# Channel mix's second product in the search rounds: three products of rounded parts, in portions by pairs of chunks

## The chip, the cores and the metric

The kernel runs on one core of a Trainium2 chip. The metric is the time of one execution on the device in microseconds (us), as the median of several runs. Engine names in the profile: PE is TensorE (PEld its weight loads), DVE is VectorE, ACT is ScalarE, POOL is GpSimd, SP is SyncE.

## The reference, cut to what matters

The input is 16 sequences of 512 tokens with 256 channels. Each token goes through an RWKV block, and beside it through a mixture of 8 experts whose SiLU gates the block's output. The part that is changed is channel mix:

```
xk2 = h2 * cmk + shift(h2) * (1 - cmk)
kf  = square(relu(xk2 @ Wfk.T))        # 1024 hidden channels
kv  = kf @ Wfv.T                       # the second product, 1024 -> 256
x   = x + sigmoid(xr2 @ Wfr.T) * kv
```

Beside the blocks the kernel routes tokens: each expert takes its 1024 most probable tokens, and for that the threshold of each expert is searched bit by bit.

## The kernel before, in words

A block is one sequence of 512 tokens; there are 16 (NB). The kernel goes through rounds 0 to 15. In round b each engine works on three blocks at once: channel mix of block b - 1, the output projection and second norm of block b, and the first norm, mixes and projections of block b + 1. Rounds 3 to 11 also carry the routing: round 3 the softmax, rounds 4 to 10 (BIT_ROUND to SELECT_ROUND - 1) four bits of the threshold search each, round 11 (SELECT_ROUND) the choice of tokens. From round 12 (LIST_ROUND) on GpSimd writes the sorted token list with indirect DMAs. After round 15 the expert stage follows.

Each engine executes its own instructions in the order in which they are written; engines wait for each other on semaphores. The order within a round is written out by hand in each engine's round_. On TensorE it is: hidden (channel mix's first product, L937 to L944, eight chunks of 128 hidden channels, each of which ScalarE takes out of psM by a ReLU, L642), the bit search's small matmul (sum_bit, L837), receptance (L956), turn1 (transposes for block b + 1, L870), channel_out portion 0 (L968), project_out (L919), projections of k and v (L905), channel_out portion 1, turn2, projection of r, channel_out portions 2 and 3.

Portion j of channel_out is a quarter of the tokens over all eight chunks, in full precision, which needs two instructions for each of its eight matmuls; portion 0 waits until all eight chunks are squared (sq_done, L646). Its result is in psKV; VectorE takes it in the next round (gate_out, L1542).

VectorE's round is: state scans (L1453), embedding (L1558, L1563), a bit test (try_bit, L1210 to L1217), L1460, L1542, statistics (L1375, L1379), L1549, the recurrence's mixes (L1471 to L1500), a bit test, the token-shift mixes (L1392, L1396), the residual after the output projection (L1533), statistics, a bit test, L1396, scans (L1439 to L1447), a bit test, and the second block's mixes (L1392, L1396, L1431). ScalarE's round is logs (L620), ReLUs and squares with the Tanh pairs (L626, L629) between them, the first norm (norm1, L545), more ReLUs and squares, affine1 (L553), the Tanh of the receptance (L654), taking the projections (L592, L590), the second norm, norm0 (L536), affine2, Exp (L603), L598, the rounded copies of the mix (L635), Exp (L608). GpSimd's round is rstd1 and rstd2 only: four small operations of 4 elements a partition each (L441, L442, L444, L446), on which norm1 and norm2 wait.

The first product already works with rounded parts: the high part is a copy to the type float32r (mix_hi), the low part is the difference (mix_lo), and hi x hi, hi x lo and lo x hi are summed. The expert stage's second product does the same with 256 columns (L1062 to L1064).

Of the kernel before, what the change touches and what calls it, by code (L numbers as in the profile page):

```python
# [27 lines left out]
F32 = mybir.dt.float32  # L28
I32 = mybir.dt.int32
F32R = mybir.dt.float32r  # L30
ALU = mybir.AluOpType
ACT = mybir.ActivationFunctionType
# [3 lines left out]
P = 128  # L36
ROUTER_ROUNDS = 3
BIT_ROUND = 4
SELECT_ROUND = BIT_ROUND + 7
LIST_ROUND = SELECT_ROUND + 1  # L40
# [30 lines left out]
def rwkv_times_moe(nc, x, xT, vec, ln0_w, ln0_b, WkT, WvT, WrT, WoT, WfkT, WfrT, WfvT, Wg, W1, W2,  # L71
                   consts, tile_iota, token_ids, pad_rows, sorted_list, xs_rows, out):
    T, C = x.shape
    SEQ = 512
    NB = T // SEQ
# [16 lines left out]
    with ExitStack() as ctx:  # L92
# [7 lines left out]
        def same_place(name, words, other, first=0):  # L100
            return nc.alloc_sbuf_tensor_at(name, [P, words], F32R, offset=home[other] + 4 * first)
# [50 lines left out]
        def part(n):  # L152
            at[0] += n
            assert at[0] <= ARENA
            return arena[:, at[0] - n:at[0]]
# [15 lines left out]
        x_in_at = at[0]  # L171
        x_in = part(J * C).rearrange("p (j c) -> p j c", j=J)
        mixB_r = part(CH * SEQ).rearrange("p (c t) -> p c t", c=CH)
        kf2 = part(HC * SEQ).rearrange("p (h t) -> p h t", h=HC)
        moe_end = at[0]
        sigf = part(J * C)
        wfr = part(CH * C).rearrange("p (k n) -> p k n", k=CH)
        wfk = kf2.rearrange("p h t -> p (h t)")[:, 0:CH * HID].rearrange("p (k n) -> p k n", k=CH)
        wfv = part(HC * C).rearrange("p (k n) -> p k n", k=HC)
        xa = [desk[:, i * 1024:(i + 1) * 1024].rearrange("p (j c) -> p j c", j=J) for i in range(2)]  # L180
        xta = [desk[:, 2048 + i * 1024:3072 + i * 1024].rearrange("p (k t) -> p k t", k=CH) for i in range(2)]
        ra = 4096
# [63 lines left out]
        h1_ready mix1_step mix1_done mixr1_done proj_done kvr_ready wkv_step pre_done relu2_done exp_done att_done o_done  # L246
        state_done log_done gap_done past_done now_done
        x2_done ln2_step ln2_stats cf2_ready hn2_ready tr2_done h2_ready mix2_step mixk_done mixk_hi wfk_hi_done mix2_done mixr2_done
        kf_done relu_done sq_done fr_done sigf_done kv_done s_done s_mult rstd1_step rstd2_step
        rows_zeroed s_idx_ready xn_done turned w1_taken xn_taken h_done gelu_done h_hi_done h_lo_done y_done tanh_done  # L250
        combine_step combined""".split()
        names += [f"{n}{i}" for n in ("gathered", "s_gathered") for i in range(RING)] + [f"rows_out{i}" for i in range(RING)]
# [6 lines left out]
        def wait_run(eng, s, value):  # L259


            eng.wait_ge(s, value)
            if not isinstance(value, int):
                eng.sem_inc(S["waited"])
# [129 lines left out]
        def _(pool):  # L394
# [60 lines left out]
            def zero_rows():  # L455
# [2 lines left out]
                    ins = pool.memset(rows[i], 0.0)  # L458
                ins.then_inc(S["rows_zeroed"], 1)

            def round_(b, listing=False, ahead=True):
                if ahead:
                    rstd1(b + 1)
                if listing:
                    add_to_list(b, 0)
                if not ahead:
                    add_to_list(b, 1)
                rstd2(b)
                if not ahead:
                    zero_rows()  # L470
                if listing and ahead:
                    add_to_list(b, 1)
# [7 lines left out]
                norm_scales(b + 1, 4 * b, 4 * b + 3)  # L480
                rstd2(b)
            norm_scales(ROUTER_ROUNDS + 1, NB - 4, NB - 1)
            with pool.Fori(ROUTER_ROUNDS, LIST_ROUND) as b:
                round_(b)
            round_(LIST_ROUND, listing=True)
            with pool.Fori(LIST_ROUND + 1, NB - 1) as b:
                round_(b, listing=True)
# [41 lines left out]
        def _(act):  # L529
# [33 lines left out]
            def affine1(b):  # L563

                if not (isinstance(b, int) and b < 2):
                    wait_run(act, S["mixr2_done"], b - 1)
                affine(b, "tr1_done", "ln1_w", "ln1_b", "h1_ready")

            def norm2(b):

                if not (isinstance(b, int) and b == NB - 1):
                    wait_run(act, S["tr1_done"], b + 2)
                norm(b, cf2, "cf2_ready", "hn2_ready")
# [26 lines left out]
            def exp_past(b):  # L600

                wait_run(act, S["pre_done"], b * CH + CH)
                act.activation(E1, E1, ACT.Exp).then_inc(S["exp_done"], 1)  # L603
# [6 lines left out]
            def keep_logits(k):  # L610

                act.wait_ge(S["logits_done"], 4 * k + 4)
                act.activation(logits[:, k * 4 * J * E:(k + 1) * 4 * J * E], psR[:, 0:4 * J * E], ACT.Copy
                               ).then_inc(S["logits_kept"], 1)
# [29 lines left out]
            def square(b, h):  # L644
                act.wait_ge(S["relu_done"], b * HC + (h + 1))
                act.activation(kf2[:, h], kf2[:, h], ACT.Square).then_inc(S["sq_done"], 1)  # L646

            def sigmoid_fr(b):

                if not (isinstance(b, int) and b == 0):  # L650
                    wait_run(act, S["s_done"], b)
                for u in range(2):
                    act.wait_ge(S["fr_done"], 2 * b + (u + 1))
                    act.activation(sigf[:, u * 512:(u + 1) * 512], psM[:, (HC + u) % 3, :],  # L654
                                   ACT.Tanh, scale=0.5).then_inc(S["sigf_done"], 1)

            def relus(b, *chunks):
                for h in chunks:
                    relu(b, h)

            def squares(b, *chunks):
                for h in chunks:
                    square(b, h)

            def round_(b, ffn=True, ahead=True, softmax=False, further=True):
                logs(b)
                if not ffn:
                    keep_logits(0)
                if ffn:
                    for h in range(2):  # L670
                        relus(b - 1, h)
                        squares(b - 1, h)
                    relus(b - 1, 2)
                shares(b)
                if ffn:
                    relus(b - 1, 3, 4)
                    squares(b - 1, 2)
                    relus(b - 1, 5)
                if ahead:
                    norm1(b + 1)  # L680
                if ffn:
                    relus(b - 1, 6)
                    squares(b - 1, 3)
                    relus(b - 1, 7)
                    squares(b - 1, 4, 5, 6, 7)
                if softmax:
                    act.wait_ge(S["route_exp_in"], 1)
                    act.activation(probs, logits, ACT.Exp).then_inc(S["route_exp_out"], 1)
                if ahead:
                    affine1(b + 1)  # L690
                if isinstance(b, int) and b == 1:
                    keep_logits(2)
                if ffn:
                    sigmoid_fr(b - 1)
                else:
                    act.wait_ge(S["weights_in"], 16 * 3)
                    act.activation(wfk_hi[:], wfk, ACT.Copy).then_inc(S["wfk_hi_done"], 1)
                if ahead:
                    take_kvr(b + 1, 0, 2)
                if not ffn:  # L700
                    keep_logits(1)
                norm2(b)
                if ahead:
                    take_kvr(b + 1, 2, 4)
                    if further:
                        norm0(b + 2)
                affine2(b)
                if ahead:
                    exp_past(b + 1)
                    take_kvr(b + 1, 4, 5)  # L710
                    exponents(b + 1)
                split_mix(b, 0)
                split_mix(b, 1)
                if ahead:
                    exp_now(b + 1)
                    take_kvr(b + 1, 5, 6)
# [14 lines left out]
            for b in range(1, ROUTER_ROUNDS):  # L731
                round_(b)
            round_(ROUTER_ROUNDS, softmax=True)
            with act.Fori(BIT_ROUND, NB - 2) as b:
                round_(b)
            round_(NB - 2, further=False)
            round_(NB - 1, ahead=False)
# [70 lines left out]
        def _(pe):  # L808
# [160 lines left out]
                                    wfv[:, h, :], start=(h == 0), stop=(h == HC - 1))  # L969
                ins.then_inc(S["kv_done"], 1)  # L970

            def round_(b, extra, ffn=True, ahead=True):
                if ffn:
                    hidden(b - 1, extra, b)
                    receptance(b - 1)
                else:
                    extra(b, 0)
                if ahead:
                    turn1(b + 1)
                if ffn and ahead:  # L980
                    channel_out(b - 1, 0)
                project_out(b)
                if ffn and not ahead:
                    channel_out(b - 1, 0)
                extra(b, 1)
                if ahead:
                    project(b + 1, 0, 1)
                if ffn:
                    channel_out(b - 1, 1)
                turn2(b)  # L990
                extra(b, 2)
                if ahead:
                    project(b + 1, 2)
                if ffn:
                    channel_out(b - 1, 2)
                extra(b, 3)
                if ffn:
                    channel_out(b - 1, 3)
# [14 lines left out]
                round_(b, router_point)  # L1013
            round_(ROUTER_ROUNDS, softmax)
            with pe.Fori(BIT_ROUND, SELECT_ROUND) as b:
                round_(b, sum_bit)
            round_(SELECT_ROUND, route)
            with pe.Fori(LIST_ROUND, NB - 1) as b:
                round_(b, nothing)
            round_(NB - 1, nothing, ahead=False)  # L1020
# [709 lines left out]
```

## Time and profile before

| what | value |
|---|---|
| median of 3 runs | 1076.61 us (1076.31 to 1077.09) |
| the profiled execution | 1077.64 us |
| its span in the profile | 1075.8 us |
| PE busy | 1015.7 us, 94% |
| DVE busy | 882.0 us, 82% |
| ACT busy | 689.6 us, 64% |
| POOL busy | 383.4 us, 36% |

Busy shares are averages over stages; what bounds a round is read from the waits in it. A row of the timeline gives start and length in us, engine, line and operation, output and input, and how many instructions the row merges; brackets give the idle time before it and who ended it. A full-precision matmul appears as two instructions.

### The profile page before, as it was taken

The numbers are of one execution on the slowest core, as the hardware profiler recorded it, in microseconds if no ns is written. First come the engines' busy times: TensorE is split into PE (matmuls) and PEld (weight loads), VectorE is DVE, ScalarE is ACT, GpSimd is POOL, SyncE is SP. The second block draws the span as 40 slices with busy tenths as digits, with TensorE's granted clock in tenths as the row PEclk, the third lists the DMA queues.
The fourth block names the chain that finished last, engine by engine and source line by source line (L and its number), as shares of the span: only waits on it lengthen the run. The fifth ranks groups of instructions, "written<-read, shape, count | busy, mean of one in ns | idle before, by whom it ended". The sixth has DMA issues, their size and how long they took to land.

```text
span 1075.8 us, 18544 instructions
## 1 busy us (share of the span) xinstructions
PE 1015.7 (94%) x5410; PEld 832.7 (77%) x5410; DVE 882.0 (82%) x1763; ACT 689.6 (64%) x1231; POOL 383.4 (36%) x407
## 2 busy tenths in 40 slices
PE   4899999899999999999999969999999999999996
PEld 4578787677777767777776757777788999999996
DVE  5899898998988889898899987887665777777775
ACT  2558567585857658585765557595555666666663
POOL 3204055110101021010101045656762776666663
PEclk9889999999999999999999989999999999999998
DMA  7544320101102010110101020124361433333320
GB/s 257 168 141 120 98 79 20 40 7 54 58 0 58 0 58 15 43 58 0 58 0 59 1 59 1 59 68 129 120 223 40 122 122 114 113 114 109 108 67 21
DMA packets 59473, 80.28 MB, mean 75 GB/s; under 512 B 7678, under 2 KB 46719, under 8 KB 59394
## 3 DMA queue, kind: packets, MB, share of 16 engines
q1 hardware_dynamic: 48130, 54.16, 15.9%
q0 software_dynamic: 11280, 25.32, 7.9%
q8 instruction: 35, 0.57, 0.2%
q14 instruction: 28, 0.23, 0.1%
HBM read 64.38 MB, written 26.36 MB: 84 GB/s over the span
## 4 chain that ended last, share of the span: by engine, by line
PE 59%; DVE 19%; issue 9%; ACT 7%; POOL 4%; DMA 1%; DVEq 1%; SPq 0%; ACTq 0%; POOLq 0%
PE psKV L968 12%; PE psM L1042 11%; PE psM L905 11%; PE psM L919 5%; DVE arena L1453 2%; DVE arena L1396 2%; ACT arena L646 2%; PE psT L870 2%; ACT arena L545 2%; DVE bnst L1375 2%; PE psM L937 2%; PE psM L956 2%; PE psKV L1062 2%; POOL cf L444 2%; PE psKV L1064 1%
## 5 line engine op out<-in xcount | busy, mean ns | idle before, releaser
L968 PE MATMUL psKV<-arena 128*128 128x256 f32 x1024 | 231.2, 380 | 2.6 <-ACT arena L646 2.6
L968 PEld LDWEIGHTS psKV<-arena 128*128 128x128 f32 x1024 | 192.7, 190 | 42.0 <-issue 17.5
L441 POOL TENSOR_SCALAR lnw<-mv 128x4 f32<-128x4 f32 x32 | 19.0, 593 | 519.2 <-DVE mv L1379 519.2
L1042 PE MATMUL psM<-arena 128*128 128x128 f32 x1136 | 139.5, 276 | 1.5 <-DVE arena L1630 1.4
L1042 PEld LDWEIGHTS psM<-arena 128*128 128x128 f32 x1136 | 132.2, 192 | 3.2 <-DVE arena L1630 2.5
L937 PE MATMUL psM<-mix_hi,wfk_hi 128*128 128x512 f32 x256 | 107.8, 421 | 21.2 <-ACT arena L642 21.2
L592 ACT ACTIVATE arena<-psM 128x512 f32<-128x512 f32 x64 | 36.5, 588 | 127.9 <-PE psM L905 127.9
L1396 DVE SCALAR_TENSOR_TENSOR arena<-arena,vecs 128x512 f32<-128x512 f32 x160 | 109.9, 745 | 0.1
L507 POOL DMA_INDIRECT out_dram<-arena,list_sb x71 | 86.5, 1218 | 59.1 <-DVE arena L1661 50.4
L545 ACT ACTIVATE arena<-s_ring,cf 128x256 f32 (+1 forms) x128 | 66.4, 591 | 59.9 <-POOL cf L446 59.9
L939 PE MATMUL psM<-mix_hi,wfk_lo 128*128 128x512 f32 x256 | 102.3, 400 | 0.0
L642 ACT ACTIVATE arena<-psM 128x512 f32<-128x512 f32 x128 | 73.7, 587 | 28.9 <-PE psM L944 26.4
L768 ACT ACTIVATE arena<-psM 128x512 f32<-128x512 f32 x71 | 42.5, 599 | 63.2 <-PE psM L1042 63.2
L434 POOL DMA_INDIRECT sorted_list<-info_cur,place_cur x64 | 73.7, 1151 | 22.3 <-issue 20.6
L944 PE MATMUL psM<-mix_lo,wfk_hi 128*128 128x512 f32 x256 | 80.9, 398 | 0.0
L937 PEld LDWEIGHTS psM<-mix_hi,wfk_hi 128*128 128x128 f32 x256 | 49.7, 194 | 36.5 <-ACT arena L642 26.8
L646 ACT ACTIVATE arena<-arena 128x512 f32<-128x512 f32 x128 | 75.2, 624 | 1.0
L494 POOL DMA_INDIRECT arena<-xs_rows,list_sb x62 | 65.9, 1063 | 21.0 <-issue 18.6
L956 PE MATMUL psM<-arena 128*128 128x256 f32 x256 | 60.4, 383 | 4.6 <-ACT arena L642 4.6
L905 PE MATMUL psM<-arena,wk 128*128 128x512 f32 x128 | 61.5, 626 | 0.5 <-DVE arena L1396 0.5
L919 PE MATMUL psM<-wo,arena 128*128 128x256 f32 x256 | 59.4, 386 | 0.7 <-DVE arena L1500 0.5
L1392 DVE TENSOR_TENSOR arena<-arena 128x512 f32<-128x512 f32 x64 | 41.7, 688 | 22.0 <-ACT arena L553 21.9
(212 smaller groups left out, 2368.4 us busy)
## 6 DMA issues: line engine op xcount, KB each, us to landing
arena<-in_x SPq DMA_DIRECT2D x16, 512.0 KB, 4.1
desk<-in_xT SPq DMA_DIRECT2D x16, 512.0 KB, 4.1
xs_rows<-s_ring SPq DMA_DIRECT2D x16, 512.0 KB, 3.2
xs_rows<-in_x SPq DMA_DIRECT2D x16, 512.0 KB
desk<-in_x SPq DMA_DIRECT2D x15, 512.0 KB, 5.0
desk<-in_W SPq DMA_DIRECT2D x8, 512.0 KB, 8.4
arena<-in_W SPq DMA_DIRECT2D x8, 512.0 KB, 7.3
out_dram<-arena,list_sb POOLq DMA_INDIRECT x71, 2.7
```

Of the source, the lines that this page charges most:

```text
L507: pool.indirect_dma_start(out[:, :], bass.IndirectOffsetOnAxis(list_sb[:, t, 0:1], axis=0), out_t[i], None, bounds_check=T - 1, oob_is_err ...
L545: ins = act.activation(hn[:, j], xs[:, j * C:(j + 1) * C], ACT.Identity, scale=cf[:, 0, j:j + 1], bias=cf[:, 1, j:j + 1])
L646: act.activation(kf2[:, h], kf2[:, h], ACT.Square).then_inc(S["sq_done"], 1)
L905: ins = pe.matmul(psM[:, u % 3, :], w[:, k, c * P:(c + 1) * P], mixA[:, m, k, :], start=(k == 0), stop=(k == CH - 1))
L919: ins = pe.matmul(psM[:, 1 + j // 2, (j % 2) * C:(j % 2 + 1) * C], att[:, c, j * P:(j + 1) * P], wo[:, c, :], start=(c == 0), stop=(c == C ...
L937: pe.matmul(psM[:, h % 3, :], wfk_hi[:, k, n], mix_hi[:, k, :], start=(k == 0), stop=False)
L939: pe.matmul(psM[:, h % 3, :], wfk_lo[:, k, n], mix_hi[:, k, :], start=False, stop=False)
L944: ins = pe.matmul(psM[:, h % 3, :], wfk_hi[:, k, n], mix_lo[:, k, :], start=False, stop=(k == CH - 1))
L956: ins = pe.matmul(psM[:, (HC + u) % 3, (j % 2) * C:(j % 2 + 1) * C], mixB_r[:, k, j * P:(j + 1) * P], wfr[:, k, :], start=(k == 0), stop=( ...
L968: ins = pe.matmul(psKV[:, j // 2, (j % 2) * C:(j % 2 + 1) * C], kf2[:, h, j * P:(j + 1) * P], wfv[:, h, :], start=(h == 0), stop=(h == HC ...
L1042: ins = pe.matmul(psM[:, t % 2, f * P:(f + 1) * P], w1_t[t % 2][:, k, f * P:(f + 1) * P], xnT[t % 2][:, k, :], start=(k == 0), stop=(k == ...
L1396: return v.scalar_tensor_tensor(dst[:, c], dmix[:, c], vecs[:, c, V[m]:V[m] + 1], hT[:, c, 0:SEQ], ALU.mult, ALU.add)
```

## The change

In rounds 4 to 11 (so for blocks 3 to 10) channel_out is replaced by channel_part. Portion p is now a pair of hidden chunks (2p, 2p + 1) over all 512 tokens. It has 24 matmuls of 256 columns: for each of four token groups and two chunks hi x hi and hi x lo, then, behind a second wait, lo x hi. Each portion waits for its own high part (ScalarE, take_hi: one copy of 128x1024 to float32r) and its own low part (GpSimd, take_lo: one subtraction of 128x1024). The low part replaces the chunk in place; the high part goes to four slots in desk. The weights wfv are split once: ScalarE copies the high part in round 3, GpSimd subtracts in place (128x2048) once round 3's product is done, and adds the parts together again (128x2048) once round 11's product is done; TensorE waits for that at the start of round 12. ScalarE's squares 4 to 7 move from behind ReLU 7 to places after the receptance's Tanh and after the first two projections.

```diff
+            def take_lo(b, p):
+                wait_run(pool, S["kf_hi_done"], (b - BIT_ROUND) * J + (p + 1))
+                n, slot = slice(2 * p, 2 * p + 2), 2 * (p % 2)
+                pool.tensor_tensor(kf_lo[:, n], kf2[:, n], kf_hi[:, slot:slot + 2].bitcast(F32), ALU.subtract
+                                   ).then_inc(S["kf_lo_done"], 1)
+
+            def split_wfv():
+                pool.wait_ge(S["wfv_hi_done"], 1)
+                pool.wait_ge(S["kv_done"], J * ROUTER_ROUNDS)
+                pool.tensor_tensor(wfv_lo, wfv, wfv_hi.bitcast(F32), ALU.subtract).then_inc(S["wfv_lo_done"], 1)
+
+            def join_wfv():
+                pool.wait_ge(S["kv_done"], J * SELECT_ROUND)
+                pool.tensor_tensor(wfv, wfv_lo.bitcast(F32), wfv_hi.bitcast(F32), ALU.add).then_inc(S["wfv_whole"], 1)
+
+            def parts_round(b):
+                rstd1(b + 1)
+                take_lo(b, 0)
+                take_lo(b, 1)
+                rstd2(b)
+                take_lo(b, 2)
+                take_lo(b, 3)
...
-            with pool.Fori(ROUTER_ROUNDS, LIST_ROUND) as b:
-                round_(b)
+            round_(ROUTER_ROUNDS)
+            split_wfv()
+            with pool.Fori(BIT_ROUND, LIST_ROUND) as b:
+                parts_round(b)
+            join_wfv()
...
+            def take_hi(b, p):
+                act.wait_ge(S["sq_done"], b * HC + (2 * p + 2))
+                act.wait_ge(S["kv_done"], b * J + (p - 1))
+                slot = 2 * (p % 2)
+                act.activation(kf_hi[:, slot:slot + 2], kf2[:, 2 * p:2 * p + 2], ACT.Copy).then_inc(S["kf_hi_done"], 1)
...
+                if parts:
+                    take_hi(b - 1, 0)
                 if ahead:
                     norm1(b + 1)
                 if ffn:
                     relus(b - 1, 6)
                     squares(b - 1, 3)
                     relus(b - 1, 7)
-                    squares(b - 1, 4, 5, 6, 7)
+                    if not parts:
+                        squares(b - 1, 4, 5, 6, 7)
...
+                if parts:
+                    squares(b - 1, 4, 5)
+                    take_hi(b - 1, 1)
                 if ahead:
                     take_kvr(b + 1, 0, 2)
...
+                if parts:
+                    squares(b - 1, 6, 7)
+                    take_hi(b - 1, 2)
                 norm2(b)
...
                     exp_past(b + 1)
+                    if parts:
+                        take_hi(b - 1, 3)
                     take_kvr(b + 1, 4, 5)
...
+            def channel_part(b, p):
+                if p == 0:
+                    pe.wait_ge(S["wfv_lo_done"], 1)
+                    wait_run(pe, S["s_mult"], b)
+                done = b * J - (BIT_ROUND - 1) * J + (p + 1)
+                pe.wait_ge(S["kf_hi_done"], done)
+                out = lambda j: psKV[:, j // 2, (j % 2) * C:(j % 2 + 1) * C]
+                for j in range(J):
+                    for h in (2 * p, 2 * p + 1):
+                        hi = kf_hi[:, h % 4, j * P:(j + 1) * P]
+                        pe.matmul(out(j), hi, wfv_hi[:, h, :], start=(h == 0 and j % 2 == 0), stop=False)
+                        pe.matmul(out(j), hi, wfv_lo[:, h, :], start=False, stop=False)
+                pe.wait_ge(S["kf_lo_done"], done)
+                for j in range(J):
+                    for h in (2 * p, 2 * p + 1):
+                        ins = pe.matmul(out(j), kf_lo[:, h, j * P:(j + 1) * P], wfv_hi[:, h, :],
+                                        start=False, stop=(h == HC - 1 and j % 2 == 1))
+                ins.then_inc(S["kv_done"], 1)
...
             with pe.Fori(BIT_ROUND, SELECT_ROUND) as b:
-                round_(b, sum_bit)
-            round_(SELECT_ROUND, route)
+                round_(b, sum_bit, channel_out=channel_part)
+            round_(SELECT_ROUND, route, channel_out=channel_part)
+            pe.wait_ge(S["wfv_whole"], 1)
```

## Rows read from the trace of the kernel before

**Rows 1.** The page, busy time and share of the span by engine.
```profile
PE 1015.7 (94%) x5410; PEld 832.7 (77%) x5410; DVE 882.0 (82%) x1763; ACT 689.6 (64%) x1231; POOL 383.4 (36%) x407
```

**Rows 2.** Timeline of VectorE, first instruction of four rounds: start, length, what.
```profile
415.43 2.33 DVE L1453 TENSOR_TENSOR_SCAN arena<-arena 128x512 f32<-128x512 f32 x2
462.33 2.33 DVE L1453 TENSOR_TENSOR_SCAN arena<-arena 128x512 f32<-128x512 f32 x2
556.11 2.33 DVE L1453 TENSOR_TENSOR_SCAN arena<-arena 128x512 f32<-128x512 f32 x2
607.04 2.33 DVE L1453 TENSOR_TENSOR_SCAN arena<-arena 128x512 f32<-128x512 f32 x2
```

**Rows 3.** Waits, 418 to 465 us: who for whom, total, times, longest.
```profile
ACT arena L545 <- POOL cf L446: 3.1, 2, 1.9
DVE s_ring L1533 <- PE psM L919: 2.0, 1, 2.0
DVE desk L1210 <- PE psR L837: 0.9, 1, 0.9
PE psM L937 <- ACT arena L642: 0.7, 1, 0.7
PE psM L956 <- ACT arena L642: 0.5, 1, 0.5
PE psKV L968 <- ACT arena L646: 0.3, 1, 0.3
```

**Rows 4.** Timeline of TensorE in round 8, an old portion, what follows, and the next round's first product.
```profile
450.84 3.62 PE L968 MATMUL psKV<-arena 128*128 128x256 f32 x16
454.29 1.04 PE L870 MATMUL psT<-cst,arena 128*128 128x128 f32 x8
...
465.76 0.58 PE L937 MATMUL psM<-mix_hi,wfk_hi 128*128 128x512 f32 x1
```

**Rows 5.** Timeline of TensorE in the expert stage, first and tenth of ten products.
```profile
902.96 0.28 PE L1063 MATMUL psKV<-w_lo,hT_h 128*128 x1
...
904.02 0.28 PE L1063 MATMUL psKV<-w_lo,hT_h 128*128 x1
```

**Rows 6.** Timeline of ScalarE in round 8.
```profile
445.89 0.60 ACT L592 ACTIVATE arena<-psM 128x512 f32<-128x512 f32 x1 [6.88 <-PE psM L905]
456.79 1.05 ACT L603 ACTIVATE arena<-arena 128x1024 f32<-128x1024 f32 x1
```

**Rows 7.** Timelines of GpSimd in rounds 0 and 3, and of VectorE beside it.
```profile
11.24 0.20 POOL L425 TENSOR_TENSOR info<-desk,info 128x4 f32<-128x4 f32 x1
149.85 2.10 POOL L413 TENSOR_TENSOR desk<-desk,info 128x16 f32<-128x16 f32 x1
150.58 1.28 DVE L1500 SCALAR_TENSOR_TENSOR arena<-arena 128x512 f32<-128x512 f32 x2
152.32 0.23 POOL L416 TENSOR_TENSOR desk<-desk,info 128x16 f32<-128x16 f32 x1
185.95 0.22 POOL L424 TENSOR_TENSOR stats<-desk,stats 128x16 f32<-128x16 f32 x1
```

**Rows 8.** Groups of instructions of GpSimd, one line: busy, mean ns of one.
```profile
L458 POOL MEMSET arena<- 128x512 f32 x9 | 4.2, 523 | 0.0
```

**Rows 9.** Timeline of VectorE in round 8.
```profile
420.42 0.14 DVE L1210 TENSOR_SCALAR desk<-desk 128x1 int32<-128x1 int32 x1
428.25 1.28 DVE L1474 SCALAR_TENSOR_TENSOR arena<-arena 128x512 f32<-128x512 f32 x2
436.50 0.14 DVE L1210 TENSOR_SCALAR desk<-desk 128x1 int32<-128x1 int32 x1
457.26 1.29 DVE L1392 TENSOR_TENSOR arena<-arena 128x512 f32<-128x512 f32 x2
```

**Rows 10.** Waits of VectorE, 556 to 607, and of TensorE, 607 to 663.
```profile
DVE s_ring L1533 <- PE psM L919: 1.6, 1, 1.6
PE psM L937 <- ACT arena L642: 10.0, 1, 10.0
```

More of the change, by code:

```diff
@@ L173, in rwkv_times_moe @@
         mixB_r = part(CH * SEQ).rearrange("p (c t) -> p c t", c=CH)
+        kf_at = at[0]
         kf2 = part(HC * SEQ).rearrange("p (h t) -> p h t", h=HC)
@@ L178, in rwkv_times_moe @@
         wfk = kf2.rearrange("p h t -> p (h t)")[:, 0:CH * HID].rearrange("p (k n) -> p k n", k=CH)
+        wfv_at = at[0]
         wfv = part(HC * C).rearrange("p (k n) -> p k n", k=HC)
+        kf_lo = same_place("kf_lo", HC * SEQ, "arena", kf_at).rearrange("p (h t) -> p h t", h=HC)
+        wfv_lo = same_place("wfv_lo", HC * C, "arena", wfv_at).rearrange("p (k n) -> p k n", k=HC)
+        kf_hi = same_place("kf_hi", 4 * SEQ, "desk").rearrange("p (h t) -> p h t", h=4)
+        wfv_hi = same_place("wfv_hi", HC * C, "desk", 4 * SEQ).rearrange("p (k n) -> p k n", k=HC)
         xa = [desk[:, i * 1024:(i + 1) * 1024].rearrange("p (j c) -> p j c", j=J) for i in range(2)]
@@ L248, in rwkv_times_moe @@
         x2_done ln2_step ln2_stats cf2_ready hn2_ready tr2_done h2_ready mix2_step mixk_done mixk_hi wfk_hi_done mix2_done mixr2_done
-        kf_done relu_done sq_done fr_done sigf_done kv_done s_done s_mult rstd1_step rstd2_step
+        kf_done relu_done sq_done kf_hi_done kf_lo_done wfv_hi_done wfv_lo_done wfv_whole fr_done sigf_done kv_done s_done s_mult rstd1_step rstd2_step
         rows_zeroed s_idx_ready xn_done turned w1_taken xn_taken h_done gelu_done h_hi_done h_lo_done y_done tanh_done
@@ L646, in square, with split_wfv @@
                 act.activation(kf2[:, h], kf2[:, h], ACT.Square).then_inc(S["sq_done"], 1)
+            def take_hi(b, p):
[3 more added lines that the diff above has]
+                act.activation(kf_hi[:, slot:slot + 2], kf2[:, 2 * p:2 * p + 2], ACT.Copy).then_inc(S["kf_hi_done"], 1)
+            def split_wfv():
+                act.wait_ge(S["logits_done"], NB)
+                act.wait_ge(S["a_step"], 2 * NB)
+                act.activation(wfv_hi, wfv, ACT.Copy).then_inc(S["wfv_hi_done"], 1)
             def sigmoid_fr(b):
@@ L663, in squares, with round_ @@
                     square(b, h)
-            def round_(b, ffn=True, ahead=True, softmax=False, further=True):
+            def round_(b, ffn=True, ahead=True, softmax=False, further=True, parts=False):
                 logs(b)
@@ L690, in round_ @@
                     affine1(b + 1)
+                if softmax:
+                    split_wfv()
                 if isinstance(b, int) and b == 1:
@@ L733, in _ @@
             round_(ROUTER_ROUNDS, softmax=True)
-            with act.Fori(BIT_ROUND, NB - 2) as b:
+            with act.Fori(BIT_ROUND, LIST_ROUND) as b:
+                round_(b, parts=True)
+            with act.Fori(LIST_ROUND, NB - 2) as b:
                 round_(b)
@@ L970, in channel_out, with round_ @@
                 ins.then_inc(S["kv_done"], 1)
-            def round_(b, extra, ffn=True, ahead=True):
+            def channel_part(b, p):
[16 more added lines that the diff above has]
+                ins.then_inc(S["kv_done"], 1)
+            def round_(b, extra, ffn=True, ahead=True, channel_out=channel_out):
                 if ffn:
```

## The prediction

> **What bounds the kernel now.** I read the busy shares first: TensorE is busy 94% of the span and VectorE 82%, so both are near the limit and neither name alone says what a saving is worth [rows 1]. Then the timeline of the state scans (L1453), which open a round on VectorE: the changed rounds 4 to 10 repeat in 46.9 us (415.43 to 462.33), round 11 takes 50.9 (556.11 to 607.04) [rows 2]. Then the waits inside round 8. TensorE waits 0.7, 0.5 and 0.3 us, each time for ScalarE; VectorE waits 2.0 us for the output projection (L919) and 0.9 us for the counting matmul [rows 3]. So a round is a loop in which TensorE has 1.5 us of slack and VectorE 2.9 us. A VectorE round that waits for no other engine lasts 46.9 - 2.9 = 44.0 us; that is the floor of the round if only TensorE gets faster, and it is the sum that matters if something is added to VectorE.
>
> **TensorE, removed and added.** One portion of the old product is 16 full-precision instructions in 3.45 us (L968 at 450.84, the next line at 454.29) [rows 4]; four portions are 13.8 us a round. The new one is 96 rounded products with 256 columns. The expert stage has the same form: nine of them start within 904.02 - 902.96 = 1.06 us, 0.118 each [rows 5]. 96 x 0.118 = 11.3 us. TensorE saves 2.5 us a round, and the 0.3 us wait for the squares goes as well, since portion 0 needs only two chunks. That is the nearest row and the lower end; the upper end is one old instruction of 256 columns, 3.45 / 16 = 0.216, by which 96 would take 20.7 (rival 4).
>
> How much of that reaches the round? VectorE's residual (L1533), from which the second norm follows, waits for the output projection, ahead of which only portion 0 has become shorter: 3.45 + 0.3 - 24 x 0.118 = 0.9 us. The other portions lie behind waits: with TensorE early, its chunks 6 and the receptance wait for ScalarE's ReLUs, which are behind the Tanh pair and the first norm, both fed by VectorE and GpSimd. So 0.9 us a round is what the faster product can give, not 2.5.
>
> **ScalarE, added.** Four copies of 128x1024 a round. The nearest row is Exp on the same size, 1.05 us [rows 6]; 4.2 us. ScalarE waits twice a round for a norm's scales from GpSimd, 3.1 us together, the longer 1.9 [rows 3]. Copy 0 falls into the shorter, 1.2 us, so nothing. Squares 4 and 5 and copy 1 (2.1 us) move into the 6.88 us idle ahead of 445.89 [rows 6]; squares 6 and 7 and copy 2 (2.1 us) into the 1.9 ahead of the second norm, 0.2 too long, which I leave out. Only copy 3 stands on the way to the mix's high part and the second Exp: up to 1.05, which the 0.9 us gained ahead of it about pays. If that cover were gone it would cost 1.05 a round. The round-3 copy of the weights (2048 elements, about 2 us) also falls into the 6.88.
>
> **GpSimd, added.** Each round has four subtractions of 128x1024; once come two passes over 128x2048 of weights (the split in round 3 to 4, the join between rounds 11 and 12). No row shows such a size. Two-tensor operations that nothing disturbs take 0.20 us for 4 elements a partition and 0.22 to 0.23 for 16 [rows 7]: 1.7 to 2.5 ns an element, so 1.9 to 2.7 us for 1024. The memset, which only writes, gives a lower end: 523 ns for 512, 1.05 us for 1024 [rows 8]. I take 2.1 us for the part that moves data, the middle of the slopes. On its own queue this is harmless: low part 0 can start at 430.9 and TensorE asks for it some 7 us later, and the second norm's scales are asked for (447) 3 us after pass 1 would end.
>
> **The port between VectorE and GpSimd.** This is what decides. At 149.85 GpSimd starts a two-tensor product of 16 elements; the same kind takes 0.23 us at 152.32, this one takes 2.10 and ends at 151.95. In between VectorE ran an unbroken row of instructions with two SBUF operands, the last two of them from 150.58 to 151.86 [rows 7]: GpSimd was through when they were. So the two engines exclude each other for VectorE instructions with two SBUF operands. The trace shows GpSimd as the loser; its own accesses there are too short to show what VectorE loses. A pass over 1024 elements is not short. If VectorE waits for it, each pass costs VectorE 2.1 us; nothing below zero is possible, since it takes no work from VectorE. Do they meet? On the old clock, each behind its copy: pass 0 at about 430.9 (where the 1.2 us wait ends), inside the stretch of two-operand instructions from 428.25 to 436.50; pass 1 at 441 (445.89 - 6.88 + 2.1), inside the mixes; pass 2 at 449 (the second take of the projection, near 447, + 2.1), ahead of mixes and scans; pass 3 at 458 (the first Exp, 456.79, + 1.05), behind L1392 at 457.26 [rows 6, 9]. All four meet.
>
> VectorE then: 44.0 + 4 x 2.1 = 52.4 us a round, and its two waits (2.9 us) are used up in that. Rounds 4 to 10: 7 x (52.4 - 46.9) = 38.5. Round 11 has 1.6 us of waiting left [rows 10]: 8.4 - 1.6 = 6.8. The two passes over the weights, 4.2 us each, start while VectorE is in the scans and embedding: 8.4. Sum 53.7. For TensorE the join costs nothing: it waits 10.0 us in round 12 as it is [rows 10].
>
> The Trainium skill (SBUF — State Buffer, section "SBUF: two separate sides") states a rule against this change: the pair of ports is an exclusive lock, held for the whole instruction by whichever began first, and a VectorE instruction with two SBUF inputs takes part against a GpSimd one that reads SBUF. The trace agrees for the half it can show (2.10 instead of 0.23 us); by that rule the sum is the one above, and without it the time would be the 1070 of the third rival. The skill's page GPSIMD Engine Reference, section 3.1, gives 4497 ns for a GpSimd addition of 2048 elements; by that a pass over 1024 would be 2.25 us, and the sum, an estimate, some 5 us more.
>
> **Forecast.** The profiled execution took 1077.64 us (span 1075.8), 1.0 above the median of the runs, 1076.61. 1077.6 + 53.7 = 1131.3; less the 1.0, 1130. Own range: with 1.9 us a pass 7 x 4.7 + 6.0 + 7.6 = 46.5, with 2.7 us 7 x 7.9 + 9.2 + 10.8 = 75: 1123 to 1152.
>
> **Rivals.**
> 1. VectorE keeps the port and GpSimd starves. For: that is all the trace shows. Against: in a long pass GpSimd only has to get in once. Place: pass 3, asked for at 458, meets two-operand work until the next round's bit test at 467.3 (420.42 + 46.9), gets about 1.7 us (the bit test has one operand), and ends at about 470.7; TensorE's last eight products then end at 471.6, and the first hidden chunk starts there instead of at 465.76 [rows 4]: 5.8 us. Pass 0 gets 1.7 us at 436.5 and ends after the mixes that follow, some 3 us late for the output projection. Together 6 to 9, I take 8: 8 x 8 = 64, 1141. Slower too.
> 2. The lock is held for less, at the memset's rate of 1.05 us: 44.0 + 4.2 = 48.2, 7 x 1.3 + 2.6 + 4.2 = 15.9: 1092. It decides from 0.72 us a pass on (2.9 / 4): below that VectorE's waits swallow it.
> 3. The other side: long passes and VectorE run past each other. Then 0.9 us x 8 = 7: 1069 to 1070. Against it stands 2.10 us for 0.23.
> 4. The change does not make the product cheaper: at 0.216 a product TensorE needs 46.9 - 1.5 + 20.7 - 13.8 = 52.3 a round: 8 x 5.4 = 43, 1120, with TensorE as the bound. Against it: the expert stage's 0.118.
>
> **Chances.** Forecast 0.50, rival 1 0.16, rival 2 0.14, rival 3 0.16, rival 4 0.04. A change of 0.2% (2.2 us) is about what can be told from none. Slower holds all but rival 3: 0.84; of the 0.16, 0.03 is for an end within 0.2%, as copy 3 takes the gain back, and 0.13 for faster. The range for 8 in 10 leaves out rival 3 and a few hundredths above: 1084 to 1150.
>
> **What would show it.** In the changed kernel: GpSimd rows of 128x1024 of 2 us or more; two-operand VectorE rows beside them longer by about 2 us or preceded by gaps that no semaphore ends, four a round; VectorE's wait at L1533 gone; scans about 52 us apart; products 0.118 apart, 2.8 us a portion. Scans 46 us apart with GpSimd rows of 2 us would prove me wrong, and a GpSimd row of 9 us with TensorE waiting for it would be rival 1.

## The result and the profile after

| what | before | after |
|---|---|---|
| median of 4 runs | 1076.46 us | 1129.36 us (1129.07 to 1130.0) |
| ratio | | 1.0492, 95% interval 1.0474 to 1.0511 |
| span of the profiled execution | 1075.8 us | 1127.3 us |

The forecast was 1130 us. The page of the changed kernel, busy time by engine, answers to [rows 1]:

```profile
PE 1018.3 (90%) x5666; PEld 836.2 (74%) x5666; DVE 957.1 (85%) x1763; ACT 720.1 (64%) x1264; POOL 479.4 (43%) x441
```

TensorE's busy time has hardly changed, VectorE's has risen by 957.1 - 882.0 = 75 us, and VectorE executes the same 1763 instructions. The timeline of VectorE, first instruction of rounds 8, 9, 11, 12 and 13 (start, length, what), answers to [rows 2]:

```profile
440.72 2.33 DVE L1531 TENSOR_TENSOR_SCAN arena<-arena 128x512 f32<-128x512 f32 x2
493.08 2.33 DVE L1531 TENSOR_TENSOR_SCAN arena<-arena 128x512 f32<-128x512 f32 x2
597.95 2.33 DVE L1531 TENSOR_TENSOR_SCAN arena<-arena 128x512 f32<-128x512 f32 x2
659.26 2.33 DVE L1531 TENSOR_TENSOR_SCAN arena<-arena 128x512 f32<-128x512 f32 x2
714.53 2.34 DVE L1531 TENSOR_TENSOR_SCAN arena<-arena 128x512 f32<-128x512 f32 x2
```

Rounds 5 to 10 last 52.4 us each (46.9 before), round 11 lasts 61.3 (50.9), round 12 lasts 55.3. Round 4, from 226.96 to 283.58, lasts 56.6. Over the old lengths this is 9.7 + 6 x 5.5 + 10.4 - 0.7 = 52.4, the whole difference of the spans (51.5) and 0.9 that the kernel is ahead when round 4 starts (226.96, before 227.83). TensorE's granted clock is lower than before, 0.964 instead of 0.981 as a mean. That is not the cause: VectorE no longer waits for TensorE (below), and e7 is 17 us slower at 0.98.

Where it is lost shows at GpSimd's passes; three of them stand here, the last of round 7 and the first two of round 8, from the timelines of GpSimd and VectorE, in order of time:

```profile
434.24 2.81 POOL L470 TENSOR_TENSOR kf_lo<-arena,kf_hi 128x1024 fp32r<-128x1024 f32 x1 [6.48 <-ACT kf_hi L684]
434.72 4.88 DVE L1474 SCALAR_TENSOR_TENSOR arena<-arena,vecs 128x512 f32<-128x512 f32 x4
...
455.90 3.31 POOL L470 TENSOR_TENSOR kf_lo<-arena,kf_hi 128x1024 fp32r<-128x1024 f32 x1
456.99 3.37 DVE L1561 SCALAR_TENSOR_TENSOR arena<-arena 128x512 f32<-128x512 f32 x2
460.29 1.28 DVE L1567 SCALAR_TENSOR_TENSOR arena<-arena 128x512 f32<-128x512 f32 x2
...
466.45 2.67 POOL L470 TENSOR_TENSOR kf_lo<-arena,kf_hi 128x1024 fp32r<-128x1024 f32 x1 [7.24 <-ACT kf_hi L684]
466.84 4.83 DVE L1474 SCALAR_TENSOR_TENSOR arena<-arena,vecs 128x512 f32<-128x512 f32 x4
```

Undisturbed, in round 12 of the same kernel, the same instructions take (timeline of VectorE):

```profile
683.41 1.27 DVE L1561 SCALAR_TENSOR_TENSOR arena<-arena 128x512 f32<-128x512 f32 x2
690.65 2.73 DVE L1474 SCALAR_TENSOR_TENSOR arena<-arena,vecs 128x512 f32<-128x512 f32 x4
```

The two instructions of L1561 take 3.37 us instead of 1.27: 2.1 us more, while GpSimd's subtraction (L470) runs. The four of L1474 take 4.88 and 4.83 instead of 2.73. The loser is not always VectorE: the row at 455.90 is 3.31 us long, where undisturbed subtractions take 2.35 (e6), and VectorE's scans end at 457.0, 1.1 us after its start. So the subtraction waits for the second scan first; once it is in, VectorE stands.

What the engines wait for in round 8 (who for whom, total, times, longest), all of VectorE's from 440.7 to 493 and the relevant ones of the others from 432 to 484, answers to [rows 3]:

```profile
DVE desk L1295 <- DVE desk L1293: 0.7, 4, 0.2
DVE s_ring L1641 <- DVE arena L1636: 0.4, 1, 0.4
...
PE psM L963 <- DVE arena L1474: 2.5, 1, 2.5
ACT mix_hi L667 <- DVE arena L1474: 2.0, 1, 2.0
```

VectorE waits for no other engine any more (the two waits left are for its own results, and the kernel before has them too); both of its waits for TensorE are gone, and TensorE and ScalarE wait for it.

The timelines of GpSimd and VectorE in round 4 show the price on a very small instruction, while GpSimd splits the weights (L476, 128x2048):

```profile
231.36 5.17 POOL L476 TENSOR_TENSOR wfv_lo<-arena,wfv_hi 128x2048 fp32r<-128x2048 f32 x1 [17.02 <-PE psKV L1026]
232.33 4.22 DVE L1291 TENSOR_TENSOR desk<-desk 128x1 f32<-128x1 f32 x1
```

One element a partition, but two operands in SBUF: 4.22 us, where the same instruction (L1213 before) takes 0.16 in all 29 bit tests before.

### The profile page after: what moved, and what is told of

The parts are those of the page before. It is cut to its first block, busy times and chain, and to the rows that moved or that the text cites. A ratio compares the mean times of both kernels' runs of the same rounds, so it can differ in the third digit from the quotient of the medians.

```text
span 1127.3 us, 19230 instructions
## 1 busy us (share of the span) xinstructions
PE 1018.3 (90%) x5666; PEld 836.2 (74%) x5666; DVE 957.1 (85%) x1763; ACT 720.1 (64%) x1264; POOL 479.4 (43%) x441
## 4 chain that ended last, share of the span: by engine, by line
PE 49%; DVE 27%; issue 14%; ACT 4%; POOL 3%; DVEq 1%; DMA 1%; SPq 0%; ACTq 0%; POOLq 0%
PE psM L1120 11%; PE psKV L1026 6%; PE psM L963 6%; DVE arena L1474 5%; PE psM L977 4%; PE psM L1014 3%; DVE bnst L1453 2%; DVE arena L1531 2%; PE psM L995 2%; DVE arena L1517 2%; PE psM L997 2%; PE psM L1002 2%; PE psT L928 2%; PE psKV L1140 1%; PE psKV L1142 1%
## 5 line engine op out<-in xcount | busy, mean ns | idle before, releaser
L995 PE MATMUL psM<-mix_hi,wfk_hi 128*128 128x512 f32 x256 | 112.0, 437 | 50.0 <-ACT arena L674 43.9
L470 POOL TENSOR_TENSOR kf_lo<-arena,kf_hi 128x1024 fp32r<-128x1024 f32 x32 | 90.0, 2811 | 120.3 <-ACT kf_hi L684 120.3
L1474 DVE SCALAR_TENSOR_TENSOR arena<-arena,vecs 128x512 f32<-128x512 f32 x160 | 139.7, 930 | 0.1
L1026 PE MATMUL psKV<-arena 128*128 128x256 f32 x512 | 114.4, 379 | 0.2 <-ACT arena L678 0.2
L1026 PEld LDWEIGHTS psKV<-arena 128*128 128x128 f32 x512 | 96.6, 190 | 18.3 <-issue 5.7
L997 PE MATMUL psM<-mix_hi,wfk_lo 128*128 128x512 f32 x256 | 106.3, 415 | 0.0
L995 PEld LDWEIGHTS psM<-mix_hi,wfk_hi 128*128 128x128 f32 x256 | 52.3, 204 | 69.3 <-ACT arena L674 52.4
L963 PE MATMUL psM<-arena,wk 128*128 128x512 f32 x128 | 70.1, 695 | 20.1 <-DVE arena L1474 19.8
L1002 PE MATMUL psM<-mix_lo,wfk_hi 128*128 128x512 f32 x256 | 84.6, 413 | 1.3 <-DVE mix_lo L1509 1.3
L826 ACT ACTIVATE arena<-psM 128x512 f32<-128x512 f32 x71 | 42.6, 601 | 62.9 <-PE psM L1120 62.9
L1040 PE MATMUL psKV<-wfv_hi,kf_hi 128*128 128x256 f32 x256 | 69.8, 313 | 0.0
L585 ACT ACTIVATE arena<-psT,vecs 128x512 f32<-128x512 f32 x64 | 46.2, 773 | 35.0 <-PE psT L928 33.0
```

What stands on the lines that cost most here:

```text
L470: pool.tensor_tensor(kf_lo[:, n], kf2[:, n], kf_hi[:, slot:slot + 2].bitcast(F32), ALU.subtract).then_inc(S["kf_lo_done"], 1)
L963: ins = pe.matmul(psM[:, u % 3, :], w[:, k, c * P:(c + 1) * P], mixA[:, m, k, :], start=(k == 0), stop=(k == CH - 1))
L995: pe.matmul(psM[:, h % 3, :], wfk_hi[:, k, n], mix_hi[:, k, :], start=(k == 0), stop=False)
L997: pe.matmul(psM[:, h % 3, :], wfk_lo[:, k, n], mix_hi[:, k, :], start=False, stop=False)
L1002: ins = pe.matmul(psM[:, h % 3, :], wfk_hi[:, k, n], mix_lo[:, k, :], start=False, stop=(k == CH - 1))
L1026: ins = pe.matmul(psKV[:, j // 2, (j % 2) * C:(j % 2 + 1) * C], kf2[:, h, j * P:(j + 1) * P], wfv[:, h, :], start=(h == 0), stop=(h == HC ...
```

## The experiments

**e1_tiny_low: the changed kernel without the length of GpSimd's passes.**

```diff
-                pool.tensor_tensor(kf_lo[:, n], kf2[:, n], kf_hi[:, slot:slot + 2].bitcast(F32), ALU.subtract
+                few = slice(0, 2)
+                pool.tensor_tensor(kf2[:, 2 * p, few], kf2[:, 2 * p, few], kf_hi[:, slot, few].bitcast(F32), ALU.subtract
...
-                        ins = pe.matmul(out(j), kf_lo[:, h, j * P:(j + 1) * P], wfv_hi[:, h, :],
+                        ins = pe.matmul(out(j), kf_hi[:, h % 4, j * P:(j + 1) * P], wfv_hi[:, h, :],
```

> The changed kernel, but each of GpSimd's four passes a round takes 2 elements a partition instead of 1024, and TensorE multiplies the high part a second time where it took the low one (so the low part of the activations is left out of the sum). All waits, copies and products stay, and the two passes over the weights. Theory L (each long GpSimd pass holds the port and VectorE stands still for 2.1 us): rounds 4 to 10 fall from 52.4 to 46.0 us (VectorE 44.0 plus what the loop adds), only the weights' 8.4 us stay: 1072 to 1080. Theory S (ScalarE's four copies, the moved squares or the new portions make the round long): nothing changes, 1125 to 1129. Theory Q (GpSimd's queue is what is waited for): faster as well, but then VectorE's rows were never longer; the trace of this run has the two-operand rows at their old lengths either way.

Measured: 1073.98 us, ratio 0.9978 (0.9969 to 0.9988). Rounds 5 to 10 last 45.5 us (411.66 to 457.17). Waits of VectorE for other engines in round 8 (columns as above):

```profile
DVE s_ring L1612 <- PE psM L978: 0.8, 1, 0.8
DVE arena L1532 <- ACT arena L641: 0.4, 2, 0.2
DVE desk L1289 <- PE psR L896: 0.3, 1, 0.3
```

Everything that the change adds to ScalarE, TensorE and the queues is still there, and the 55 us are gone: theory S falls. The wait for the output projection fell from 2.0 to 0.8, that for the counting matmul from 0.9 to 0.3, and 0.2 for the second Exp is new (the window holds the start of two rounds, so the row has it twice): 1.2 + 0.6 - 0.2 = 1.6. The round is 46.9 - 45.5 = 1.4 us shorter. That is what the faster product is worth, net of ScalarE's copies, while the low parts come for nothing.

**e2_four_passes: the passes alone, on the kernel before.** Spare memory in desk, started on semaphores that engines raise at about the times of the high parts.

```diff
+            def pass_(b, p):
+                wait_run(pool, S[("sq_done", "sigf_done", "kvr_ready", "exp_done")[p]],
+                         (b * HC - HC + 2, 2 * b, 6 * b + 8, 2 * b + 3)[p])
+                pool.tensor_tensor(desk[:, 2048 + 1024 * (p % 2):3072 + 1024 * (p % 2)], desk[:, 0:1024], desk[:, 1024:2048], ALU.subtract
+                                   ).then_inc(S["pass_done"], 1)
```

> The kernel before, nothing of the change in it, but GpSimd makes four subtractions of 128x1024 a round in rounds 4 to 11 on spare memory, at about the places of the low parts; no engine waits for them until long after round 11. Theory L: VectorE's round is 44.0 + 4 x 2.1 = 52.4 us, so 7 x 5.5 + 6.8 = 45 more: 1122 (1115 to 1128). Theories S and Q: nobody waits for these passes and ScalarE and TensorE do as before, so 1076.5.

Measured: 1118.75 us, ratio 1.0394 (1.0376 to 1.0411), rounds of 52.2 us. Timelines of VectorE and GpSimd in round 8, the round's first instruction and the last of the four passes:

```profile
434.51 2.33 DVE L1471 TENSOR_TENSOR_SCAN arena<-arena 128x512 f32<-128x512 f32 x2
...
479.43 2.36 POOL L465 TENSOR_TENSOR desk<-desk 128x1024 f32<-128x1024 f32 x1 [5.53 <-ACT arena L621]
479.66 3.29 DVE L1410 TENSOR_TENSOR arena<-arena 128x512 f32<-128x512 f32 x2
```

L1410 takes 3.29 us; undisturbed it takes 1.29. Work for which nobody waits, on an engine that was idle, costs 42.6 us. That decides between L and Q.

**e3_four_writes: the same, with writes only.**

```diff
-                pool.tensor_tensor(desk[...], desk[:, 0:1024], desk[:, 1024:2048], ALU.subtract).then_inc(...)
+                for q in range(2):
+                    ins = pool.memset(desk[:, 2048 * (p % 2) + 1024 * q:2048 * (p % 2) + 1024 * (q + 1)], 0.0)
+                ins.then_inc(S["pass_done"], 1)
```

> As e2_four_passes, but in place of each subtraction two memsets of 128x1024, which read nothing and should take about 2.1 us together. If the port is held by any GpSimd instruction: 1122 as e2. If only reading holds VectorE up: 1076.5, within 1 us, and the memset rows show 1.05 us each beside two-operand VectorE rows of the old length. I expect the second, 0.7 to 0.3.

Measured: 1074.85 us, ratio 0.9987 (0.9977 to 0.9996). Timelines of GpSimd and VectorE in round 8:

```profile
426.25 1.85 POOL L466 MEMSET desk<- 128x1024 f32 x2
426.15 2.33 DVE L1497 TENSOR_TENSOR_SCAN arena<-arena 128x512 f32<-128x512 f32 x2
```

Two memsets (1.85 us together) run beside the two scans, and those take 2.33 us as they do in every other round (two scans of the same size in [rows 2]). Only GpSimd's reading holds VectorE up. The 1.3 us under the kernel before are not the memsets' doing: e6 shows the same. Both write GpSimd's round 3 out ahead of its loop, and round 3 lasts 49.0 us in e3 instead of 50.0; why was not looked into. In the traces of e2, e5, e7 and e8 round 3 lasts 49.0 us too, so what their passes cost is about 1 us more than the difference of the medians.

**e4_vector_low: VectorE makes the low parts.**

```diff
-                take_lo(b, 0)
-                take_lo(b, 1)
...
+            def take_lo(b, p):
+                wait_run(v, S["kf_hi_done"], (b - BIT_ROUND) * J + (p + 1))
+                n, slot = slice(2 * p, 2 * p + 2), 2 * (p % 2)
+                v.tensor_tensor(kf_lo[:, n], kf2[:, n], kf_hi[:, slot:slot + 2].bitcast(F32), ALU.subtract
+                                ).then_inc(S["kf_lo_done"], 1)
```

> The changed kernel with the low parts made by VectorE itself, four instructions of 1.13 us a round placed at 1: the end of the recurrence's mixes, 2: ahead of the residual, 3: behind the scans, 4: at the round's end. The weights' passes stay with GpSimd. Theory L: VectorE needs 44.0 + 4.5 = 48.5 us a round instead of 52.4; 7 x 1.6 + 2.9 + 8.4 = 22.5 over the kernel before: 1099 (1092 to 1104). Theory S: 1129 or more. Theory Q: below the kernel before, near 1072, since no engine waits for GpSimd any more.

Measured: 1097.42 us, ratio 1.0197 (1.018 to 1.0214), rounds of 48.4 us (423.84 to 472.22). Moving the work onto the fuller engine gains 32 us over the changed kernel: VectorE does in 1.13 us what GpSimd does while keeping it standing for 2.1.

**e5_one_operand: passes with one tensor operand.**

```diff
-                pool.tensor_tensor(desk[...], desk[:, 0:1024], desk[:, 1024:2048], ALU.subtract).then_inc(...)
+                pool.tensor_scalar(desk[...], desk[:, 0:1024], 1.0, 0.0, ALU.mult, ALU.add).then_inc(...)
```

> As e2_four_passes, but each pass has one tensor operand (tensor_scalar, 128x1024). Theory L holds for any GpSimd instruction that reads: clean one-operand rows grow from 0.19 us at 4 elements to 0.21 at 16, 1.7 ns an element, 1.9 us a pass; then 44.0 + 7.6 = 51.6 a round: 1115. If one operand streams at the memset's 0.95 us per 1024: 44.0 + 3.8 = 47.8, 1088. If only a second operand goes through the port that VectorE needs: 1076. I take 1.0 us and 1088 as likeliest, since four reads would otherwise cost as much as eight.

Measured: 1080.52 us, ratio 1.0054 (1.0034 to 1.0074), rounds of 47.7 us. Timelines of GpSimd and VectorE in round 8:

```profile
438.67 1.42 POOL L465 TENSOR_SCALAR desk<-desk 128x1024 f32<-128x1024 f32 x1 [6.57 <-ACT arena L672]
438.50 2.13 DVE L1410 TENSOR_TENSOR arena<-arena 128x512 f32<-128x512 f32 x2
457.50 1.43 POOL L465 TENSOR_SCALAR desk<-desk 128x1024 f32<-128x1024 f32 x1 [6.68 <-ACT arena L621]
457.94 3.51 DVE L1414 SCALAR_TENSOR_TENSOR arena<-arena,vecs 128x512 f32<-128x512 f32 x4
```

L1410 takes 2.13 instead of 1.29 and L1414 3.51 instead of 2.73: one operand of 1024 holds VectorE for 0.8 us, two for 2.1. The round I expected at 0.95 us a pass, 47.8, is nearly the one measured; 0.8 us a pass gives 44.0 + 3.2 = 47.2, and 0.5 of the waits was left. What was too high is the step from the round to 1088: 7 x 0.9 + (3.8 - 1.6) = 8.5 makes 1085, and the 1.0 us a pass that I took makes 1087. Measured are 4.0 us over the kernel before; 1 us of what is missing is the shorter round 3.

**e6_two_in_window and e7_two_in_mixes: the same two passes at two places.** In e6 they start at the end of VectorE's mixes, in e7 right behind the first norm's scales.

```diff
+            def pass_round(b):
+                rstd1(b + 1)
+                wait_run(pool, S["mix1_done"], 2 * b + 4)      # e6 only
+                pass_(b, 0)
+                pass_(b, 1)
+                rstd2(b)
```

> The kernel before with two GpSimd subtractions of 128x1024 a round on spare memory, back to back, started when VectorE has finished the block's mixes (L1396) and so while it waits for the output projection and then works on it (one operand in PSUM), the statistics and a bit test: a window of 6.8 us for 2 x 2.1. Theory L (only two-operand VectorE instructions are held up): 1076.1, within 2 us. Theory L2 (a GpSimd pass holds up whatever VectorE runs): 2 x 2.1 less the 2.0 us wait that it covers, 8 x 2.2 = 18, 1094. I give L 0.85.

> The same two subtractions, started behind the first norm's scales, inside VectorE's stretch of two-operand instructions. Theory L: 44.0 + 4.2 = 48.2 us a round, 7 x 1.3 + 2.6 = 12: 1088 (1085 to 1091). If the number of passes and not their place decided, this and e6_two_in_window would be the same.

Measured: e6 1074.96 us, ratio 0.9987 (0.9978 to 0.9996); e7 1093.32 us, ratio 1.0159 (1.0143 to 1.0174). Timelines of both engines in round 8 of e6:

```profile
439.11 4.66 POOL L463 TENSOR_TENSOR desk<-desk 128x1024 f32<-128x1024 f32 x2 [11.69 <-DVE arena L1411]
440.89 1.22 DVE L1548 TENSOR_TENSOR s_ring<-s_ring,psM 128x1024 f32 x1 [1.96 <-PE psM L934]
442.26 1.41 DVE L1390 BATCH_NORM_STATS2 bnst<-s_ring 128x6 f32 x4
```

and of e7:

```profile
436.79 6.10 POOL L463 TENSOR_TENSOR desk<-desk 128x1024 f32<-128x1024 f32 x2
437.88 5.56 DVE L1497 SCALAR_TENSOR_TENSOR arena<-arena 128x512 f32<-128x512 f32 x2
443.36 1.28 DVE L1503 SCALAR_TENSOR_TENSOR arena<-arena 128x512 f32<-128x512 f32 x2
```

In e6 the two passes take 4.66 us for both, 2.3 each, and VectorE's residual (one operand in PSUM) and statistics beside them have their old 1.22 and 1.41. In e7 two instructions take 5.56 for 1.26: 4.3 us. The same work costs nothing or 17 us by its place. The round of e7 is 49.0 us, not the 48.2 expected: the passes lie ahead of the output projection, so only the wait for it (2.0) covers them, 46.9 + 4.3 - 2.0 = 49.2; the second wait was still there, 0.8.

**e8_short_passes: 256 elements instead of 1024, at the places of e2.**

```diff
-                pool.tensor_tensor(desk[:, 2048 + 1024 * (p % 2):3072 + 1024 * (p % 2)], desk[:, 0:1024], desk[:, 1024:2048], ALU.subtract
+                pool.tensor_tensor(desk[:, 2048 + 256 * (p % 2):2304 + 256 * (p % 2)], desk[:, 0:256], desk[:, 1024:1280], ALU.subtract
```

> The kernel before with four GpSimd subtractions a round at the places of e2_four_passes, of 256 elements a partition instead of 1024. Theory L with a price in proportion to length: 0.17 + 256 x 2.0 ns = 0.7 us each at most, 2.7 together, under VectorE's 2.9 us of waits: 1076.1 to 1079. If each pass had a fixed price (a lock taken and given back, a wait for the queue to drain), more than that: 1085 and up.

Measured: 1079.66 us, ratio 1.0034 (1.0021 to 1.0048), rounds of 47.4 us (415.36 to 462.74); that is 0.7 us above the upper end of what I expected. Timelines of GpSimd and VectorE in round 4, the scans beside a pass:

```profile
240.89 1.62 POOL L465 TENSOR_TENSOR desk<-desk 128x256 f32<-128x256 f32 x1
240.76 2.83 DVE L1496 TENSOR_TENSOR_SCAN arena<-arena 128x512 f32<-128x512 f32 x2
```

2.83 us instead of 2.33: 0.5 us for 256 elements, 2.1 for 1024. The price goes with the length and has no fixed part to speak of. Of 2.0 us a round, 0.5 shows and the waits cover the rest, where I had expected them to cover all.

**e9_placed and e10_one_in_window: an attempt at a version that is faster than both.** GpSimd makes parts 1 and 2 (e10: part 1 alone) in the window of e6, VectorE the others; the weights' passes start behind VectorE's L1460, and TensorE waits for the join at its first use.

```diff
+                wait_run(pool, S["mix1_done"], 2 * b + 4)
                 take_lo(b, 1)
+                take_lo(b, 2)                                   # not in e10
                 rstd2(b)
...
+                pool.wait_ge(S["gap_done"], CH * BIT_ROUND + CH)   # split; the join likewise in round 12
...
                     squares(b - 1, 4, 5)
                     take_hi(b - 1, 1)
+                    squares(b - 1, 6, 7)
+                    take_hi(b - 1, 2)
```

> The changed kernel with its low parts placed by theory L: GpSimd makes parts 1 and 2, started behind VectorE's mixes (the window of e6_two_in_window), for which ScalarE's squares 6 and 7 and copy 2 move up behind copy 1; VectorE makes parts 0 and 3 itself (1.13 us each). The weights' passes start when VectorE has come to the one-operand stretch behind L1460 (rounds 4 and 12), and TensorE waits for the join at its first use instead of at the round's start. Theory L: 44.0 + 2.3 = 46.3 us a round against 46.9, 8 x 0.6 = 5 less, and 1 for the weights' passes: 1072 (1069 to 1077). If the windows do not hold: 46.3 + 4.2 a round, 1105.

> As e9_placed, but only low part 1 is made by GpSimd in the window behind VectorE's mixes; VectorE makes parts 0, 2 and 3 itself. In e9_placed the second pass ran into a bit test (a two-operand instruction of one element a partition took 1.54 us instead of 0.16) and kept the second norm's scales waiting. Theory L with that reading: the one pass ends before the bit test and the scales; 44.0 + 3 x 1.13 = 47.4 us a round instead of 48.7 in e9_placed, 8 x 1.3 = 10 less: 1081 (1079 to 1086). If the pass itself is what costs in the window, 1091 as e9_placed or more.

Measured: e9 1091.14 us, ratio 1.0136 (1.012 to 1.0151); e10 1083.43 us, ratio 1.0068 (1.0045 to 1.0092). Both beat the changed kernel, neither the one before. Timelines of both engines in round 8 of e9:

```profile
451.72 4.67 POOL L471 TENSOR_TENSOR kf_lo<-arena,kf_hi 128x1024 fp32r<-128x1024 f32 x2 [13.00 <-DVE arena L1477]
451.29 1.22 DVE L1614 TENSOR_TENSOR s_ring<-s_ring,psM 128x1024 f32 x1
454.87 1.54 DVE L1294 TENSOR_TENSOR desk<-desk 128x1 f32<-128x1 f32 x1
456.47 0.19 POOL L448 TENSOR_SCALAR lnw<-mv 128x4 f32<-128x4 f32 x1
```

With TensorE early, VectorE no longer waits 2.0 us ahead of its residual, so the window is 2 us shorter than in e6, and the second pass ran over its end: the bit test's L1294 took 1.54 us for 0.16, and GpSimd came to the second norm's scales at 456.5, 1.9 us after its statistics were there. My expectation had carried e6's window over to a kernel in which it is shorter. With one pass the round is 47.3 us (e10, 417.52 to 464.78), as expected (47.4), against 48.7 in e9. What did pay is the new place of the split: round 4 of e9 lasts 50.3 us (227.16 to 277.50), 1.7 more than its neighbours, instead of 4.2 more.

## Why the prediction was right

- **VectorE's floor of 44.0 us and four passes of 2.1.** Right in its mechanism and its size. A round lasts 52.4, VectorE's waits for others are 0, and the pass costs 2.1 in the rows of the changed kernel and in e7. The size is in part luck: it was drawn from the difference of 0.02 to 0.03 us between rows of 4 and of 16 elements, which are given to 0.01 us, so slopes from 0.8 to 3.3 ns an element would have fitted them. That the price lies in GpSimd's reading and in VectorE's two-operand instructions, not in the passes' number or in a queue, is shown by e2, e3, e6 and e7 together.
- **The rule of the Trainium skill** (SBUF — State Buffer, "SBUF: two separate sides"): that the pair is held for a whole instruction by whichever began first. The runs agree that either side can lose: GpSimd's row of 3.31 us begins with a wait for a scan, and VectorE's one-element row of 4.22 us ends with the weights' pass (both at 236.5). On "whole" they differ where GpSimd has one operand: in e5 VectorE is held for 0.8 us of a row of 1.42. That writing alone does not take part is stated on the same page ("Who interferes with whom") and is shown by e3.
- **Split and join, 4.2 each.** Round 4 shows 56.6 - 52.4 = 4.2. The join ran in round 11's last mixes (two instructions of L1509, 5.58 us instead of 1.28: 4.3), ahead of round 12 where I had put it, because TensorE ended its product ahead of VectorE's round (timelines of GpSimd and VectorE there):

```profile
653.31 4.88 POOL L480 TENSOR_TENSOR arena<-wfv_lo,wfv_hi 128x2048 f32<-128x2048 f32 x1 [1.35 <-PE psKV L1045]
653.76 5.58 DVE L1509 TENSOR_TENSOR mix_lo<-arena,mix_hi 128x512 fp32r<-128x512 f32 x2
```

  With it, round 11 is 50.9 + 4 x 2.1 + 4.3 - 1.6 = 62.0 against 61.3 measured.
- **The sum, by its terms.** Rounds 4 to 10 without the split 7 x 5.5 = 38.5 (forecast 38.5), split 4.2 and join 4.3 (8.4), round 11 without the join 6.1 (6.8): 53.1 against 53.7. From that go 0.7 in round 12 and the 0.9 ahead of round 4, which the forecast did not have and whose cause was not looked into: 51.5 between the two spans. Between the medians it is 52.9.
- **TensorE's products at 0.118.** From one product to the next it is 0.12 us; rival 4 is out. But a portion's first product stands 0.5 us ahead of the second in portions 1 and 2, 0.2 in portions 0 and 3 (timeline of TensorE, portion 2 of round 7):

```profile
432.76 0.68 PE L1040 MATMUL psKV<-wfv_hi,kf_hi 128*128 128x256 f32 x1
433.28 0.28 PE L1041 MATMUL psKV<-wfv_lo,kf_hi 128*128 128x256 f32 x1
433.39 0.28 PE L1040 MATMUL psKV<-wfv_hi,kf_hi 128*128 128x256 f32 x1
...
435.98 0.28 PE L895 MATMUL psR<-desk,cst 128*128 128x1 f32 x2
```

  That portion takes 3.2 us, not 24 x 0.118 = 2.8, and the four of round 8 together 12.3 instead of 11.3: TensorE saves about 1.5 us a round, not 2.5. Why the first product is late was not looked into. What reaches the round was mis-sized the other way: the step "0.9 us a round is what the faster product can give" measured 1.4 (e1), since the second of VectorE's waits shrinks too. Neither had weight in the forecast.
- **ScalarE's copies at nothing.** e1 has them all and is 2 us faster than before. Right to within the 0.2 us a round for which VectorE waits for the second Exp in e1; copy 3 stands ahead of that Exp, but no run takes the copies out.
- **Rival 1** (GpSimd starves) is refuted: none of GpSimd's 32 subtractions takes more than 3.4 us. The prediction had the bit test down as an instruction of one operand; it has two-operand instructions as well (L1213), and one of them was held for 4.22 us. **Rival 2** (shorter hold) fails at 2.1 us, but its point of decision, VectorE's 2.9 us of waits, was optimistic: e8 loses 0.5 us a round at 2.0 in sum, e5 0.8 at 3.2. **Rival 3** is refuted by e2.

What stays open: why round 3 is 1 us shorter in the kernels with passes on spare memory, and whether a version that keeps the faster product's 1.4 us a round can make its low parts for less; e10, the best of three attempts, loses 7 us against the kernel before.

## What to carry to other kernels

An idle GpSimd is not free beside a busy VectorE. Count how many microseconds GpSimd's instruction holds (here 2.1 ns an element a partition with two operands, 0.8 with one), look at what VectorE runs then, and charge VectorE the whole of it if that has two operands in SBUF. Where VectorE added out of PSUM, took statistics of one operand, or waited, it cost nothing (e6). If an elementwise step must be done beside two-operand work, VectorE's own 1.13 us for 1024 elements is the cheaper price (e4).

## What the runs showed that was not expected

- An instruction of one element a partition with two operands is held as long as one of 512: 4.22 us for 0.16 (round 4 of the changed kernel), 1.54 for 0.16 (e9).
- GpSimd's reading of one operand holds VectorE for 0.8 us per 1024 elements while its row is 1.42 us long; with two operands it is 2.1 of 2.3. Two operands cost more than twice one, and the rows do not say why.
- GpSimd's memsets, which took 0.95 us per 1024 elements, held nothing at all (e3).
